# One decoder layer on one core: GELU calls two steps apart, GELU rounding on GpSimd, earlier reads of softmax sums

## The chip, the cores and the metric

The kernel runs on one core of one Trainium2 chip. The core has TensorE (PE in the profile; its weight loads are PEld), VectorE (DVE), ScalarE (ACT), GpSimd (POOL) and SyncE (SP), each with an instruction stream of its own, and DMA queues. The metric is the device time in microseconds, the median of several runs; lower is better.

## The reference

A batch of 16 sequences of 512 tokens with 256 features goes through attention and a feed-forward part, each with a layer norm behind it:

```
q = query @ wq + query @ Aq @ Bq * 4;  k = query @ wk;  v = query @ wv + query @ Av @ Bv * 4
q, k = rope(q), rope(k)                      # 16 heads of 16
attn = softmax(causal(q k^T / 4));  x = layernorm(query + (attn v) @ wo)
h = butterfly(x @ W_exp + b_exp, up)         # 1024 hidden, 10 stages, linear
h = gelu(h + up_bias)
y = butterfly(h, down) @ W_con + b_con + down_bias
out = layernorm(x + y)
```

The butterflies are linear, so the kernel folds them into two dense matrices, W1 (256 x 1024) and W2 (1024 x 256), once at the start.

## The kernel before, in words

All work of a batch is cut into pieces, and a function `steps` writes out by hand the order of the pieces. Every engine walks the same list and does the pieces that are its own, in order, so an engine that waits in one piece holds back all its later ones. An iteration `i` has 20 steps (`t`), and each step does the scores of one quarter of a head group; pieces of the neighbouring batches (`i+1`, `i-1`, `i-2`) are laid between them. Iterations 3 to 14 run as a loop, the rest is written out.

Products that need float32 accuracy are made of three matmul passes on rounded parts: a high part, rounded by ScalarE, and a low part, the rest, subtracted by VectorE or GpSimd (`mm3`).

The pieces that the change and the steps below touch, by name:

- S: scores of a step (L564, L590), from which VectorE takes the maxima (L869, L874); every fifth step it rounds them into `m_pad` (L883, L885), MT transposes them, ScalarE copies them to `m_row`, MOUT stores and MROW reads them back on SP (L464, L468).
- ST: the scores transposed (L602), for steps later by the lead of S; ScalarE exponentiates them into `pT` (L743), and GpSimd zeroes what lies behind the diagonal (SEL, L1026). There are three PSUM banks for two halves a step, so ST of a step waits for the first exp of the step before. PV multiplies with the values (L637).
- RAW stores a group's raw sums and outputs, SMOC reads back the sums `s_m` and the outputs `o_c` (L480, L482), RCP takes reciprocals on VectorE (L906), REC stores them (L485), RB reads them back spread over the partitions (L493), and ON multiplies on GpSimd (L1041). Each has two halves, 0 and 1; WO, the output projection (L647), needs both.
- WO's result is added to the input on VectorE (L911); LNS, LNA and LNB are the statistics, the aggregate with a power on GpSimd (L1045), and the scaling of a layer norm; BIAS adds a bias on GpSimd (L1051).
- XT transposes the normed rows (L653); ScalarE and VectorE split them (L774, L897); W1 expands (L522), and its eight tiles are read out by ScalarE (even, L820) and VectorE (odd, L914).
- GE is one GELU call over half of the hidden units (L826). GHI rounds a piece of the result (ScalarE, L794) into `x1T_hi`, GLO makes its low part (L919) in `x1T_lo`, and W2 and W2B contract the first and the second half (L669); W2E adds the rest of the layer (L933). The high and low buffers hold one piece for each half, so a piece waits for the W2 of the piece before it.
- ROPE, HIGH and LOW rotate and split the heads of the next batch (GpSimd L1035, L1036, ScalarE L770, GpSimd L373); QKH, QKL store them and FILL reads them back on SP; XRES reads the residual; XTL, XHI, XLO load and split the batch after that; V makes the values of the next batch.

Of the kernel before, what the change touches and what calls it, by code (L numbers as in the profile page):

```python
# [52 lines left out]
def steps(i, static):  # L53
# [19 lines left out]
    second = {2: ("MT", i, 1), 7: ("MT", i, 2), 12: ("MT", i, 3), 17: ("MT", i + 1, 0), 14: ("XT", i - 1, 0)}
    third = {14: ("XT", i - 1, 1)}
    for n in range(1, NHT):
        (first if n % 2 else third)[16 + (n - 1) // 2] = ("W1", i - 1, n)
    for n in range(NHT):
        (first if n > 1 else third)[2 + n] = ("W2B" if n % 2 else "W2", i - 2, n // 2)
    for t in range(NU):
# [35 lines left out]
        if t == 18:  # L115
            put("LNB", i - 2, 3)
# [25 lines left out]
        if t == 19:  # L142
            put("GE", i - 1, 1)
# [61 lines left out]
def layer(nc, xT_d, x_d, wqk_d, wv_d, lora_d, wo_d, wexpT_d, upin_d, dnin_d, wx_d, bx_d, wcon_d,  # L205
          bout_d, cs_d, ident_d, mask_d, out_d):
    ctx = ExitStack()
    with ctx:
# [623 lines left out]
        def _(dve):  # L832
# [26 lines left out]
            def one(step):  # L859
# [56 lines left out]
                elif kind == "GLO":  # L916
                    tile, half = n // 2, n % 2
                    dve.wait_ge(ghi_done, NHT * b + n + 1)
                    dve.tensor_tensor(g_lo[:, half, :, :],  # L919
                                      gact[:, NHT // 2 * half:NHT // 2 * (half + 1),  # L920
                                           tile * P:(tile + 1) * P],
                                      g_hi[:, half, :, :].bitcast(FP32), ALU.subtract)\
                       .then_inc(glo_done, 1)
# [79 lines left out]
        def _(pool):  # L1003
# [7 lines left out]
            def one(step):  # L1011
# [158 lines left out]
```

## Time and profile before

| | |
|---|---|
| median of 3 runs | 1574.66 us (1572.19 to 1581.97) |
| the profiled execution's own time | 1588.03 us |
| its span | 1586.3 us |
| PE busy | 1275.8 us, 80% |
| DVE busy | 971.9 us, 61% |
| ACT busy | 768.3 us, 48% |
| POOL busy | 491.5 us, 31% |
| mean granted clock of TensorE | 0.883 |

The span runs from the first to the last instruction of one profiled execution, which was slower than the median of the runs. Busy shares are means over the whole span. The granted clock is a share of 2.4 GHz: 0.5 is 1.2 GHz throughout a stretch, 1.0 is 2.4. A tile's name on the left of an arrow is written, on the right read; the second buffers for the GELU parts lie in those of the normed rows, so GHI and GLO carry the names `x1T_hi` and `x1T_lo`.

### The profile page before, as it was taken

To read this page: it belongs to the slowest core of one execution; us is meant where nothing else is said; L and a number is where in the kernel's file an instruction comes from. 1 tells how busy PE (TensorE), PEld (TensorE's weight loads), DVE (VectorE), ACT (ScalarE), POOL (GpSimd) and SP (SyncE) were. 2 spreads that over 40 slices of the span, in tenths; PEclk is the share of its full clock that TensorE was granted. 3 is DMA by queue.
4 is the path that set the end of the run, shared out by engine and by line. 5 is a ranking of instruction groups with operands and counts; after the bars stand their busy time and mean duration, and the time that the engine had idled before them with its cause. 6 is when DMAs were issued, how large, how long until landed. Compare 5 with 4: busy or idle time off the path is not lost.

```text
span 1586.3 us, 27377 instructions
## 1 busy us (share of the span) xinstructions
PE 1275.8 (80%) x8328; PEld 820.5 (52%) x8328; DVE 971.9 (61%) x2024; ACT 768.3 (48%) x1259; POOL 491.5 (31%) x520
## 2 busy tenths in 40 slices
PE   3677888888878888887888888788887888879766
PEld 2433445555555555555555645555555555545355
DVE  6689555665656567565656656655665666566333
ACT  1366454553636455363645536364553636464512
POOL 3124233242323324242332424233242423322210
PEclk8878899998989989898899989889898989998888
DMA  5744534253343525334342533435253343522110
GB/s 199 174 116 129 136 89 122 63 156 84 109 122 93 145 62 154 81 109 131 96 135 62 155 81 102 127 86 156 62 150 84 102 128 92 150 75 64 34 43 27
DMA packets 94983, 169.89 MB, mean 107 GB/s; under 512 B 14872, under 2 KB 36120, under 8 KB 94944
## 3 DMA queue, kind: packets, MB, share of 16 engines
q1 hardware_dynamic: 93888, 166.53, 38.3%
q10 hardware_dynamic: 832, 1.83, 0.3%
q0 software_dynamic: 224, 1.04, 0.2%
q8 instruction: 21, 0.34, 0.1%
q14 instruction: 18, 0.15, 0.0%
HBM read 92.28 MB, written 77.07 MB: 107 GB/s over the span
## 4 chain that ended last, share of the span: by engine, by line
PE 50%; issue 17%; DVE 14%; ACT 11%; DMA 4%; POOL 3%; ACTq 0%; SPq 0%; DVEq 0%; POOLq 0%
PE ps_m L522 16%; PE ps_m L669 8%; PE ps_o L637 7%; PE ps_m L647 6%; PE ps_t L602 5%; DVE m_raw L874 4%; ACT pT L743 3%; PE ps_s L564 3%; PE ps_s L590 3%; ACT L743 2%; DVE x1T_lo L919 2%; PE ps_m L653 1%; POOL o_c L1041 1%; DVE rope_in L893 1%; ACT L826 1%
## 5 line engine op out<-in xcount | busy, mean ns | idle before, releaser
L743 ACT ACTIVATE pT<-ps_t 128x512 f32<-128x512 f32 x640 | 346.9, 595 | 475.8 <-PE ps_t L602 474.7
L874 DVE TENSOR_REDUCE m_raw<-ps_s 128x1 f32<-128x512 f32 (+2 forms) x768 | 344.7, 503 | 157.0 <-PE ps_s L590 154.5
L1026 POOL TENSOR_SCALAR_AFFINE_SELECT pT<-pT 128x512 f32<-128x512 f32 (+1 forms) x320 | 188.8, 592 | 744.5 <-ACT pT L743 744.4
L602 PE MATMUL ps_t<-q_st,k_st 50*128 50x512 f32 (+3 forms) x1024 | 177.1, 405 | 75.3 <-ACT pT L743 68.6
L637 PE MATMUL ps_o<-pT,v_aug 128*32 128x512 f32 (+3 forms) x2048 | 212.8, 490 | 7.2 <-issue 7.2
L919 DVE TENSOR_TENSOR x1T_lo<-gact,x1T_hi 128x512 fp32r<-128x512 f32 x128 | 124.7, 976 | 128.5 <-ACT x1T_hi L794 126.7
L564 PE MATMUL ps_s<-k_st,q_st 48*128 48x512 f32 (+3 forms) x1024 | 142.9, 338 | 66.6 <-DVE m_raw L874 46.6
L602 PEld LDWEIGHTS ps_t<-q_st,k_st 50*128 50x128 f32 x1024 | 86.1, 195 | 176.9 <-ACT pT L743 82.2
L647 PE MATMUL ps_m<-wo,o_c 128*128 128x256 f32 x256 | 90.0, 513 | 73.2 <-POOL o_c L1041 73.2
L564 PEld LDWEIGHTS ps_s<-k_st,q_st 48*128 48x128 f32 x1024 | 103.4, 204 | 79.9 <-DVE m_raw L874 54.9
L669 PE MATMUL ps_m<-w_hi,x1T_hi 128*128 128x256 f32 x512 | 95.7, 310 | 43.1 <-DVE rope_in L893 18.8
L590 PE MATMUL ps_s<-maskb,identb 128*128 128x256 bf16 (+1 forms) x640 | 118.5, 269 | 0.0
L669 PEld LDWEIGHTS ps_m<-w_hi,x1T_hi 128*128 128x128 f32 x512 | 70.4, 193 | 87.6 <-issue 47.0
L647 PEld LDWEIGHTS ps_m<-wo,o_c 128*128 128x128 f32 x256 | 62.6, 257 | 101.0 <-POOL o_c L1041 60.3
L522 PE MATMUL ps_m<-x1T_hi,w_hi 128*128 128x512 f32 x256 | 100.2, 476 | 12.2 <-DVE x1T_lo L897 10.9
L794 ACT ACTIVATE x1T_hi<-gact 128x512 fp32r<-128x512 f32 x128 | 80.4, 630 | 56.6 <-PE ps_m L669 56.6
L911 DVE TENSOR_TENSOR x_res<-ps_m,x_res 128x512 f32<-128x512 f32 x32 | 22.1, 691 | 133.9 <-PE ps_m L647 133.9
L914 DVE TENSOR_SCALAR gact<-ps_m,gbias 128x512 f32<-128x512 f32 x64 | 48.0, 750 | 85.3 <-PE ps_m L522 85.1
L869 DVE TENSOR_REDUCE m_raw<-ps_s 128x2 f32<-128x512 f32 x128 | 81.9, 681 | 10.2 <-PE ps_s L590 9.8
L373 POOL TENSOR_TENSOR rot<-rot,rot_hi 128x1024 f32<-128x1024 f32 x28 | 66.6, 2380 | 67.9 <-ACT rot_hi L770 67.9
L820 ACT ACTIVATE gact<-ps_m,gbias 128x512 f32<-128x512 f32 x64 | 44.0, 688 | 86.4 <-PE ps_m L522 86.4
L522 PE MATMUL ps_m<-x1T_lo,w_hi 128*128 128x512 f32 x256 | 85.3, 416 | 0.0
(119 smaller groups left out, 2063.5 us busy)
## 6 DMA issues: line engine op xcount, KB each, us to landing
qk_scr<-rot_hi SPq DMA_DIRECT2D x64, 512.0 KB, 3.6
q_st<-qk_scr SPq DMA_DIRECT2D x128, 192.0 KB, 4.5
k_st<-qk_scr SPq DMA_DIRECT2D x128, 192.0 KB, 4.9
qk_scr<-rot SPq DMA_DIRECT2D x32, 512.0 KB, 3.2
o_scr<-o_raw SPq DMA_DIRECT2D x64, 256.0 KB, 2.1
r_b<-in_xT SPq DMA_DIRECT2D x17, 512.0 KB, 3.4
o_c<-o_scr SPq DMA_DIRECT2D x32, 256.0 KB
r_b<-r_scr SPq DMA_DIRECT2D x32, 256.0 KB
```

The lines of the kernel that those rows point to most:

```text
L522: mm = pe.matmul(out, w[a][k], x[c][k], start=(j == 0 and k == 0), stop=(j == 2 and k == n - 1))
L564: return pe.matmul(ps_s[:, r, off:off + (qt + 1) * P], q_st[rows, pr, qt * P:(qt + 1) * P], k_st[rows, pr, 0:(qt + 1) * P], start=start, s ...
L590: pe.matmul(o, identb[:, :], m, start=False, stop=True, skip_group_check=True).then_inc(s_done, 1)
L602: return pe.matmul(ps_t[:, ST_BANK[2 * n + r], off:off + (NT - kt) * P], k_st[rows, pr, kt * P:(kt + 1) * P], q_st[rows, pr, kt * P:T], st ...
L637: mm = pe.matmul(ps_o[32 * j:32 * j + 32, q0:q1], v_aug[:, kt, GH * g + j, :], src, start=(c == 0), stop=(c == 3), skip_group_check=True)
L647: mm = pe.matmul(pm[:, j * D:(j + 1) * D], o_c[:, k, t * P:(t + 1) * P], wo[:, k, :], start=(k == 0), stop=(k == KD - 1))
L669: mm = pe.matmul(pm[:, 0:D], (g_hi, g_lo)[a][:, half, k, :], (w2_hi, w2_lo)[c][:, NHT // 2 * half + k, :], start=(half + j + k == 0), stop ...
L743: act.activation(pT[:, g % 2, slot, half * T:(half + 1) * T], ps_t[:, ST_BANK[2 * n + r], :], ACT.Exp, scale=SCALE).then_inc(exp_done, 1)
L869: ins = dve.tensor_reduce(m_raw[:, r, :, 1], ps_s[:, r, :].rearrange("p (x c) -> p x c", x=GP), AX.X, ALU.max, negate=True)
L874: ins = dve.tensor_reduce(m_raw[:, r, u // 2, qt:qt + 1], ps_s[:, r, off:off + (qt + 1) * P], AX.X, ALU.max, negate=True)
L919: dve.tensor_tensor(g_lo[:, half, :, :], gact[:, NHT // 2 * half:NHT // 2 * (half + 1), tile * P:(tile + 1) * P], g_hi[:, half, :, :].bitc ...
L1026: pool.affine_select(out=v, in_=v, compare_op=ALU.is_ge, fill=0.0, base=0, pattern=pattern, channel_multiplier=-1).then_inc(mask_done, 1)
```

## The change

What moves, by piece (step before, step now):

- the second GELU call from behind the exps of step 19 to behind those of step 0 of the next iteration, and with it GHI, GLO, W2, W2B and W2E one step later each (W2 of the first tile 2 to 3);
- GLO from VectorE to GpSimd;
- SMOC of half 1 in front of its step's transfers, RCP and REC of half 1 from step 8 to 7, in front of LNS and of MOUT, RB of it from 8 to 7 behind MOUT, ON of it from 10 to 9, and RCP and REC of half 0 from 19 to 18; XRES of half 1 from 9 to 10;
- V from steps 10 and 13 to 13 and 14, XT from 14 to 15 with one transpose on either side of ST and S, W1 from 15 to 19 into 16 to 19, two a step;
- the first statistics (LNS) of the first layer norm ahead of WO's second result, and the last of the second from 15 to 14.

```diff
     first = {0: ("QK", i + 1, 0), 1: ("QK", i + 1, 1), 2: ("QK", i + 1, 2), 3: ("QK", i + 1, 3),
-             10: ("V", i + 1, 0), 11: ("WO", i - 1, 0), 12: ("WO", i - 1, 1), 13: ("V", i + 1, 1),
-             15: ("W1", i - 1, 0)}
...
+             11: ("WO", i - 1, 0), 12: ("WO", i - 1, 1), 13: ("V", i + 1, 0), 14: ("V", i + 1, 1),
+             15: ("XT", i - 1, 0)}
...
-        if 1 <= t <= NHT:
-            put("GHI", i - 2, t - 1)
-            put("GLO", i - 2, t - 1)
+        if 2 <= t < 2 + NHT:
+            put("GHI", i - 2, t - 2)
+            put("GLO", i - 2, t - 2)
         if t == 6:
-            put("LNS", i - 2, 2)
-        if t == 8:
+            put("SMOC", i - 1, 1)
+        if t == 7:
             put("RCP", i - 1, 1)
             put("REC", i - 1, 1)
+            put("LNS", i - 2, 2)
-        if t == 10:
+        if t == 9:
             put("ON", i - 1, 1)
...
         if t == 18:
             put("GE", i - 1, 0)
-        if t == 19:
-            put("GE", i - 1, 1)
+        if t == 0:
+            put("GE", i - 2, 1)
...
+                elif kind == "GLO":
+                    tile, half = n // 2, n % 2
+                    pool.wait_ge(ghi_done, NHT * b + n + 1)
+                    pool.tensor_tensor(g_lo[:, half, :, :],
+                                      gact[:, NHT // 2 * half:NHT // 2 * (half + 1),
+                                           tile * P:(tile + 1) * P],
+                                      g_hi[:, half, :, :].bitcast(FP32), ALU.subtract)\
+                       .then_inc(glo_done, 1)
```

The line numbers of the changed kernel are lower by 4 in the first half of the engines' code, and GLO stands at L1034. GpSimd in steps 2 and 3 of the loop, before (LOW, then ON; the selections are SEL):

```order
L1026 AFFINE_SELECT pT<-pT 128x2x256
L372 REGISTER_ALU
L373 TENSOR_TENSOR rot<-rot,rot_hi 128x1024
L393 ISA
L1026 AFFINE_SELECT pT<-pT 128x2x128
L1039 ISA
L1041 TENSOR_TENSOR o_c<-o_c,r_b 128x512
```

and now, from the selection of step 1 on:

```order
L1014 AFFINE_SELECT pT<-pT 128x2x256
L1033 ISA
L1034 TENSOR_TENSOR x1T_lo<-gact,x1T_hi 128x512
L368 REGISTER_ALU
L369 TENSOR_TENSOR rot<-rot,rot_hi 128x1024
L389 ISA
L1014 AFFINE_SELECT pT<-pT 128x2x128
L1033 REGISTER_ALU
L1034 TENSOR_TENSOR x1T_lo<-gact,x1T_hi 128x512
L1027 ISA
L1029 TENSOR_TENSOR o_c<-o_c,r_b 128x512
```

A subtraction of the GELU part (GLO) now stands ahead of LOW and of ON, and so on in each step to the ninth.

SyncE behind the fetches of the next batch's first group, before (steps 8 and 9: MROW's two reads, then REC, RB, XRES):

```order
L468 DMA q_st<-m_scr 2x1024
L468 ISA
L468 DMA q_st<-m_scr 2x1024
L393 REGISTER_ALU
L485 ISA
L485 DMA r_scr<-r_m 64x64
L393 REGISTER_ALU
L493 DMA r_b<-r_scr 128x1x512
L425 ISA
L425 DMA x_res<-in_x 128x2x256
```

and now (steps 6 and 7: XRES, then REC, MOUT, RB):

```order
L421 DMA x_res<-in_x 128x2x256
L389 REGISTER_ALU
L481 ISA
L481 DMA r_scr<-r_m 64x64
L389 REGISTER_ALU
L460 ISA
L460 DMA m_scr<-m_row 32x128
L389 REGISTER_ALU
L489 DMA r_b<-r_scr 128x1x512
L389 REGISTER_ALU
```

The store of the reciprocals went ahead of the maxima's store and of the fetches, and their spread read ahead of the fetches and of the maxima's reads.

ScalarE at the end of the loop, before (the exps of step 18, GELU, the exps of step 19, GELU):

```order
L743 ACTIVATE pT<-ps_t 128x512
L819 REGISTER_ALU
L820 ACTIVATE gact<-ps_m,gbias 128x512
L826 ACT_TABLE_LOAD
L826 ACTIVATE gact<-gact 128x2048
L742 ISA
L743 ACT_TABLE_LOAD
L743 ACTIVATE pT<-ps_t 128x512
L742 REGISTER_ALU
L743 ACTIVATE pT<-ps_t 128x512
L826 ACT_TABLE_LOAD
L826 ACTIVATE gact<-gact 128x2048
```

and now at the loop's head (behind the copy OE of the outputs: the exps of step 0, GELU, the first exp of step 1):

```order
L738 ISA
L739 ACTIVATE pT<-ps_t 128x512
L738 REGISTER_ALU
L739 ACTIVATE pT<-ps_t 128x512
L820 ISA
L822 ACT_TABLE_LOAD
L822 ACTIVATE gact<-gact 128x2048
L738 ISA
L739 ACT_TABLE_LOAD
L739 ACTIVATE pT<-ps_t 128x512
```

The second call left the end of the loop and stands one step's exps, and the copy of the outputs, further on.

## Rows read from the trace of the kernel before

**Rows 1.** Windows: one iteration; us, busy (x count) PE, PEld, DVE, ACT, POOL, clock, DMA.

```profile
778.80:871.60 92.80, 77.27 (x516) 49.97 (x516) 58.21 (x120) 46.36 (x76) 30.57 (x32) 0.91 0.40 109
```

**Rows 2.** Table of waits, whole run: who <- whom: us in total, times, longest.

```profile
PE ps_m L647 <- POOL o_c L1041: 73.2, 16, 6.1
...
PE ps_t L602 <- ACT pT L743: 68.6, 33, 3.8
...
PE ps_s L564 <- DVE m_raw L874: 46.6, 30, 3.6
...
PE ps_m L669 <- DVE rope_in L893: 18.8, 13, 1.9
...
PE ps_m L669 <- DVE x1T_lo L919: 17.2, 30, 4.3
```

**Rows 3.** Timeline, steps 6 to 11: start, us, engine, line, what; idle before, releaser.

```profile
715.36 0.67 SPq L480 DMA_DIRECT2D s_m<-o_scr  x1
...
719.77 0.54 DVE L906 RECIPROCAL r_m<-s_m 64x64 f32<-64x64 f32 x1
...
723.33 0.66 SPq L468 DMA_DIRECT2D q_st<-m_scr  x2
...
724.32 0.59 SPq L485 DMA_DIRECT2D r_scr<-r_m  x1
...
727.03 0.67 SPq L493 DMA_DIRECT2D r_b<-r_scr  x1
...
731.14 1.26 POOL L1041 TENSOR_TENSOR o_c<-o_c,r_b 128x512 f32<-128x512 f32 x1 [5.84 <-DMA r_b<-r_scr]
...
732.45 3.43 PE L647 MATMUL ps_m<-wo,o_c 128*128 128x256 f32 x8 [4.97 <-POOL o_c L1041]
```

**Rows 4.** Timeline around the GELU calls, one iteration and the end of another.

```profile
689.80 0.55 PE L602 MATMUL ps_t<-q_st,k_st 50*128 50x128 f32 x4 [3.15 <-ACT pT L743]
...
771.35 1.92 ACT L826 ACTIVATE gact<-gact 128x2048 f32<-128x2048 f32 x1
...
775.71 0.50 PE L602 MATMUL ps_t<-q_st,k_st 50*128 50x512 f32 x2 [1.42 <-ACT pT L743]
...
776.97 1.91 ACT L826 ACTIVATE gact<-gact 128x2048 f32<-128x2048 f32 x1
```

**Rows 5.** Windows, columns as in rows 1, of three stretches behind holes.

```profile
690.00:697.30 7.30, 6.08 (x31) 2.85 (x29) 6.34 (x11) 4.00 (x9) 4.05 (x4) 0.77 0.73 144
732.40:736.00 3.60, 3.55 (x12) 2.68 (x12) 0.00 (x0) 0.00 (x0) 0.36 (x1) 0.58 0.78 170
750.60:755.00 4.40, 4.40 (x15) 2.98 (x16) 0.50 (x2) 1.44 (x3) 0.00 (x0) 0.50 0.75 174
```

**Rows 6.** By line: GpSimd and VectorE (ns min/median/max; the page's rows: busy, mean).

```profile
L1036 POOL TENSOR_TENSOR rot<-rope_in x32: 1258/1282/1745, 21.9 to 1353.5; 128x512 f32<-128x512 f32 x32
...
L919 DVE TENSOR_TENSOR x1T_lo<-gact,x1T_hi x128: 677/692/2470, 225.9 to 1575.7; 128x512 fp32r<-128x512 f32 x128
...
L1026 POOL TENSOR_SCALAR_AFFINE_SELECT pT<-pT 128x512 f32<-128x512 f32 (+1 forms) x320 | 188.8, 592 | 744.5 <-ACT pT L743 744.4
...
L373 POOL TENSOR_TENSOR rot<-rot,rot_hi 128x1024 f32<-128x1024 f32 x28 | 66.6, 2380 | 67.9 <-ACT rot_hi L770 67.9
```

**Rows 7.** Timeline: first W2 matmuls of step 4 and of step 7.

```profile
704.56 0.73 PE L669 MATMUL ps_m<-w_hi,x1T_hi 128*128 128x256 f32 x4 [0.42 <-DVE y L933]
...
714.89 0.73 PE L669 MATMUL ps_m<-w_hi,x1T_hi 128*128 128x256 f32 x4 [0.49 <-DVE x1T_lo L919]
```

**Rows 8.** Timeline: S behind the layer norm, and the first W1.

```profile
747.19 0.50 PE L564 MATMUL ps_s<-k_st,q_st 48*128 48x512 f32 x2 [2.11 <-DVE m_raw L874]
...
750.59 1.19 PE L522 MATMUL ps_m<-x1T_hi,w_hi 128*128 128x512 f32 x2 [0.79 <-DVE x1T_lo L897]
```

**Rows 9.** Timeline: GpSimd's addition and VectorE's cast beside it.

```profile
757.97 2.42 POOL L1051 TENSOR_TENSOR x_res<-x_res,bias_out 128x1024 f32<-128x1024 f32 x1
...
759.25 1.18 DVE L883 CAST m_pad<-m_raw 128x16 fp32r<-128x16 f32 x1
```

More of the change, by code:

```diff
@@ L70, in steps @@
     first = {0: ("QK", i + 1, 0), 1: ("QK", i + 1, 1), 2: ("QK", i + 1, 2), 3: ("QK", i + 1, 3),
-             10: ("V", i + 1, 0), 11: ("WO", i - 1, 0), 12: ("WO", i - 1, 1), 13: ("V", i + 1, 1),
-             15: ("W1", i - 1, 0)}
[L73 to L76, printed above, removed]
+             11: ("WO", i - 1, 0), 12: ("WO", i - 1, 1), 13: ("V", i + 1, 0), 14: ("V", i + 1, 1),
+             15: ("XT", i - 1, 0)}
+    second = {2: ("MT", i, 1), 7: ("MT", i, 2), 12: ("MT", i, 3), 17: ("MT", i + 1, 0), 15: ("XT", i - 1, 1)}
+    third = {3: ("W2", i - 2, 0)}
     for n in range(NHT):
-        (first if n > 1 else third)[2 + n] = ("W2B" if n % 2 else "W2", i - 2, n // 2)
+        (third if n % 2 else first)[16 + n // 2] = ("W1", i - 1, n)
+        if n:
+            first[3 + n] = ("W2B" if n % 2 else "W2", i - 2, n // 2)
     for t in range(NU):
@@ L93, in steps @@
                 put("MROW", b, n)
-        if 1 <= t <= NHT:
-            put("GHI", i - 2, t - 1)
-            put("GLO", i - 2, t - 1)
+        if 2 <= t < 2 + NHT:
+            put("GHI", i - 2, t - 2)
+            put("GLO", i - 2, t - 2)
         if t == 6:
-            put("LNS", i - 2, 2)
-        if t == 8:
+            put("SMOC", i - 1, 1)
+        if t == 7:
             put("RCP", i - 1, 1)
             put("REC", i - 1, 1)
-        if t == 10:
+            put("LNS", i - 2, 2)
+        if t == 9:
             put("ON", i - 1, 1)
+        if t == 12:
+            put("LNS", i - 1, 0)
         if t == 13:
@@ L108, in steps @@
             put("LNB", i - 1, 1)
-        if t == 15:
             put("LNS", i - 2, 3)
@@ L115, in steps @@
         if t == 18:
+            put("RCP", i, 0)
+            put("REC", i, 0)
             put("LNB", i - 2, 3)
@@ L122, in steps @@
         if t == 12:
-            put("LNS", i - 1, 0)
             put("LNS", i - 1, 1)
@@ L131, in steps @@
                     put("MOUT", table[t][1], table[t][2])
-                if table[t][0] == "W2B":
-                    put("W2E", *table[t][1:])
         if u >= 1:
@@ L155, in steps @@
         if t == 6:
-            put("SMOC", i - 1, 1)
             put("XRES", i - 1, 0)
         if t == 7:
+            put("RB", i - 1, 1)
             put("FILL", i + 1, 0)
-        if t == 8:
-            put("RB", i - 1, 1)
-        if t == 9:
+        if t == 10:
             put("XRES", i - 1, 1)
-        if t == 10:
             put("FILL", i + 1, 1)
@@ L178, in steps @@
             put("OUT", i - 2)
-            put("RCP", i, 0)
-            put("REC", i, 0)
         put("SEL", i, t)
@@ L915, in one @@
                        .then_inc(evac_w1[1], 1)
[L916 to L923, printed above, removed]
                 elif kind == "DM":
```

## The prediction

> **What bounds the kernel now.** I read the busy times by iteration first, then the table of waits, then the timeline of one iteration. One iteration of the steady loop (one batch) takes 92.8 us, of which TensorE's matmuls are busy 77.3, VectorE 58.2, ScalarE 46.4 and GpSimd 30.6 [rows 1]. TensorE is the bound, with 15.5 us of holes per batch, and some of its busy time is run at a lower clock. The table of waits names the holes over the whole run: 73.2 us (16 times, once a batch) in which the output projection WO waits for GpSimd's scaled `o_c`, 68.6 us (33 times, two a batch) in which the transposed scores ST wait for a score bank that ScalarE's exps have not read, 46.6 us in which the scores S wait for the maxima, and 36.0 us (18.8 and 17.2) ahead of the contracting matmuls W2 [rows 2]. Of the 15.5 us a batch these are nearly all.
>
> The timeline shows how the two large ones come about. WO: the sums are read back at 715.36, the reciprocal runs at 719.77, but its store is issued only at 724.32, behind the transfers of the maxima rows at 723.33 in SP's order; the spread reciprocals are fetched at 727.03, GpSimd multiplies at 731.14 to 732.40, and WO starts at 732.45 after a wait of 4.97 [rows 3]. GELU: two calls of 1.9 us with a table load on either side start at 771.35 and 776.97, with just one step's exps between them; ST waits 1.42 at 775.71, and, at the same place of the iteration before, 3.15 at 689.80 for the second [rows 4]. After each large hole the granted clock is low: 0.77 over 690.0 to 697.3 and 0.58 over 732.4 to 736.0, so part of that time is at 1.2 GHz instead of 2.4, after TensorE had stood idle [rows 5].
>
> **The change part by part.**
>
> *Reads of sums and reciprocals (SMOC, RCP, REC, RB, ON).* Nothing is added; the same transfers go earlier. From the read of the sums to the end of the multiply the chain took 17.0 us: 4.4 to the reciprocal, 4.55 from there to the store, 2.7 to the fetch, 4.1 to its landing [rows 3]. With the store ahead of its step's MOUT the 4.55 falls to about 0.7, since the reciprocal itself is 0.54 long; the fetch then stands behind one MOUT, worth at most a microsecond. The reciprocal is one step earlier, in front of LNS, GLO and a step's maxima, and the read of the sums no longer stands behind the last low part of the rotated heads: another 2 to 4 us. So `o_c` is ready 6 to 8 us sooner against a wait of 5, and the wait goes, with 1 to 3 us to spare. ON also stands behind the last GLO on GpSimd, which eats 1.28 of it [rows 6]. What is late next is TensorE itself, with W2 of the last tile in the place of V. Queued behind the new waits: VectorE's reciprocal now stands ahead of a step's maxima and waits for the sums; they were there 4.4 us after issue without a wait being shown, so its cost is between 0 and about 2 us a batch; I take 0, because half a step or more lies between. XRES, FILL and MROW on SP come later by the fetch's wait (RB waits some 2 us for the store); MROW is bound by its own landing, so 0 to 1 us, and I take 0. Gain: 73.2 less the last batch's 6.1, where nothing is left to cover it, 67; and the clock: 3.55 us busy at 0.58 is 3.55 x 0.42 = 1.5 us a batch [rows 5], x 15 = 22. Together **-89**.
>
> *GELU two steps apart.* The same two calls and four table loads a batch. A call with its loads holds ScalarE for 1.28 + 1.92 + 1.28 = 4.5 us. ST of a step needs the first exp of the step before, so a hole of 4.5 us after a step's exps is hidden if TensorE has more than that before the ST after the next. After the first call it has S, two W1 tiles and PV, ST, S, another W1, PV and QK: some 9 us. After the second (now behind ST of step 0) it has S, QK, ST, S, PV, QK: about 6.5. Both cover it, the second barely, so I leave 0.5 us a batch (8) and take 68.6 - 8 = 61; from 690.0 to 697.3 TensorE was busy 6.08 us at 0.77, 6.08 x 0.23 = 1.4 a batch [rows 5], x 15 = 21. Together **-82**. The price: the second half's first high part (GHI) moves a step later, and W2 with it.
>
> *Low rounding (GLO) on GpSimd.* VectorE loses 8 calls a batch of 692 ns median; GpSimd gains 8. The nearest rows are its addition of the same shape, 1282 median and 1745 at most, and its 128x1024 subtraction at 2380, half of which is 1190 [rows 6]: I take 1.28, bounds 1.19 and 1.75. GpSimd's 30.6 us a batch become 41, so it is no bound over the batch, but it is over steps 2 to 6. Between the end of the first GLO and that of the fifth, it must do in order: LOW, SEL, GLO, ON, SEL, GLO, two rotations (ROPE), SEL, GLO, LOW, SEL, GLO, which is 2 x 2.38 + 4 x 0.59 + 4 x 1.28 + 3 x 1.28 = 16.1 us, and about 1 us (an estimate) in which LOW waits for ScalarE's HIGH: 17.1. TensorE from the same point to the W2 that takes the fifth low part needs 2 us to reach the first W2 (estimate), 2.0 for it with its PV, and three steps: 704.56 to 714.89 is 10.33, less 0.49 of wait 9.84 [rows 7]: 13.8. So W2 waits some **3 us a batch** for GpSimd, x 15 = +45, bounds 0 and 6. That these 3 us also lower the clock is as likely as not (after 1.42 of wait it stayed, after 3.15 it fell): +1.4 x 15 / 2 = +11. The old waits ahead of W2, 36.0, go: the bank is free earlier and VectorE's queue is no longer in the way. In the last two iterations W2 is a bare chain, longer by 1.28 - 0.69 for each of four tiles: +5. Together **+25**.
>
> The GPSIMD Engine Reference of the Trainium skill (section Engine selection) speaks against this edit: elementwise work of two inputs belongs on VectorE and is about twice as slow on GpSimd. The trace agrees, 1282 against 692 ns, 1.85 times. At twice 692 the calls would be 0.10 us longer each, the stretch 0.4 us, the sum 6 us worse.
>
> *V later, layer norms spread (V, XT, W1, LNS).* No work changes. With V now on both sides of S1 the wait of 2.11 for the maxima behind the layer norm [rows 8] is covered by the 1.5 us of a V pair, but the S between the two transposes then waits for the statistics LNS put in front of its predecessor's maxima: I leave 1 us, a gain of 1.1 x 15 = 17. The second transpose now ends right ahead of W1, and its low part is queued on VectorE behind four maxima (1.4 us) : the wait of 0.79 [rows 8] becomes some 1.7, x 15 = +14, bounds 0 and 2.5 a batch. The slow stretch behind it (0.50 over 750.6 to 755.0 [rows 5]) I leave as it is. Together **-3**. The move of the other half's RCP and REC by a step I put at nothing: ON of that half is not what WO waits for.
>
> **The sum.** -89 - 82 + 25 - 3 = -149 against the profiled execution's own 1588.03 us (its span 1586.3 and 1.7 around it): 1439. The median of the three runs, 1574.66, is 0.9916 of the profiled time, so the forecast is 1439 x 0.9916 = **1427 us**, 9.4% less.
>
> **Rivals.**
>
> *GpSimd sets the pace more than I think.* VectorE's tiny operations on SBUF are held while GpSimd works: the 128x16 cast at 759.25, 0.17 us long elsewhere, took 1.18 and ended with GpSimd's addition of 757.97 to 760.39; a GLO of 692 ns took up to 2470 [rows 6, 9]. GpSimd will be near full in steps 2 to 8, so GLOs of 1.63 (5 x 0.35 = 1.75) and 2.4 us of held casts ahead of MT would add 4.2 us a batch, 62 in all: 1501 x 0.9916 = 1488. For it: how full those steps are; against: the longest holder, VectorE's own GLO, leaves that port. The SBUF — State Buffer page of the Trainium skill (section SBUF: two separate sides) gives the rule: the two engines' shared port pair is an exclusive lock for a whole instruction. The trace agrees, by the cast that ends with the addition. Chance 0.17.
>
> *The reciprocals are still late.* If the sums land later than the reciprocal's new place, or the fetch stays behind MOUT, half of the 89 stays: 1483.5 x 0.9916 = 1471. Chance 0.08.
>
> *The GELU hole only moves, so that the change doesn't do what it says.* The second call waits for the last W1 that VectorE adds its bias to, now behind the maxima of the last step; if that is late by 2 us, ST of step 2 waits and half of 82 stays: 1468. Chance 0.06.
>
> *Faster.* GpSimd keeps up after all (TensorE reaches W2 later than I reckon): the 45 and 11 go, 1383 x 0.9916 = 1371. Chance 0.09.
>
> *Slower than before.* One mechanism: GLO itself on GpSimd. It reads `gact` in four pieces of 128 elements, 512 apart, and writes the rounded type. Five GLOs stand in the stretch that sets the pace, so from 149 / 15 / 5 = 2.0 us more each, that is at 3.3 us, the gain is gone; at 4.0 us it is 1439 + 5 x 2.72 x 15 = 1643, x 0.9916 = 1629. Against it: SEL, with strided pieces too, takes 0.59 [rows 6]. Chance 0.02.
>
> **How the numbers follow.** The forecast has 0.58. Its own range is some 35 us either way (bounds of the W2 wait, 0 and 6 us a batch, are 45 us each way, but not all terms are at their ends together). Leaving out the outer half of the faster and the pacing rivals, the range is 1390 to 1490. Within 1% of before is what a measurement here can hardly tell from no change; it needs two or three rivals at once: 0.03. Slower by over 1%: 0.02. Faster by over 1%: 0.95.
>
> **What the new profile would show.** Right: the iteration at 81 to 84 us; WO's wait on `o_c` near 0 outside the last batch; ST's wait for exps under 10 us in all; GLO at 1.2 to 1.4 us on GpSimd, and W2's wait for it the longest hole on TensorE, 2 to 4 us a batch; W1 after the transposes waiting 1 to 2 us; the clock near 1 around WO and W2. Wrong: GLO above 1.6 us, WO still waiting for `o_c`, the wait of S or of ST's maxima rows grown by several us a batch, or VectorE's casts held at the maxima of steps 6 and 11.

## The result, and the profile after

The changed kernel took 1411.1 us, the median of 4 runs (1407.79 to 1418.86), against 1573.9 (1572.19 to 1581.97): a ratio of 0.8966, 95% interval 0.8924 to 0.9008. The forecast was 1427, 9.4% less; it is 10.3% less.

The page of the changed kernel's profile, busy time by engine:

```profile
PE 1214.9 (86%) x8328; PEld 790.2 (56%) x8328; DVE 844.4 (60%) x1896; ACT 756.9 (54%) x1259; POOL 633.5 (45%) x648
```

Windows of the changed kernel, one iteration, columns as in [rows 1]:

```profile
702.25:780.66 78.41, 71.72 (x517) 47.16 (x516) 49.25 (x112) 45.55 (x75) 39.76 (x40) 0.98 0.47 130
```

An iteration takes 78.4 us instead of 92.8 (forecast 81 to 84), at a mean clock of 0.98 instead of 0.91. TensorE runs the same number of matmuls over the same data, but is busy 60.9 us less over the run (1275.8 to 1214.9): that part of the gain is clock, the rest is waits. That it is clock shows in the product of busy time and the run's mean granted clock, which hardly moves: 1275.8 x 0.883 = 1126.5 before, 1214.9 x 0.928 = 1127.4 now. The profiled execution took 1407.79 us (span 1406.0) where that of before took 1588.03. The spans are 180.3 apart, so 119.4 of it are waits.

The waits of TensorE in the changed kernel, columns as in [rows 2]:

```profile
PE ps_m L665 <- POOL x1T_lo L1034: 44.2, 35, 4.8
PE ps_t L598 <- DMA q_st<-m_scr: 34.4, 15, 4.4
PE ps_m L518 <- DVE x1T_lo L893: 26.6, 16, 2.0
...
PE ps_s L560 <- DVE m_raw L870: 11.7, 13, 1.9
PE ps_t L598 <- ACT pT L739: 11.0, 19, 1.2
...
PE ps_m L643 <- POOL o_c L1029: 2.9, 1, 2.9
```

Against [rows 2]: WO's wait for `o_c` fell from 73.2 to 2.9, that of ST for the exps from 68.6 to 11.0, that of S for the maxima from 46.6 to 11.7. W2 waits 44.2 for GpSimd instead of 36.0 for VectorE. One large row the prediction had put at nothing: ST waits 34.4 us, once a batch, for `q_st<-m_scr`, the maxima rows MROW. In the kernel before that was 6.4.

The clock is read from the groups by line (busy, mean ns of one; then idle before them). Kernel before: the values' PV, the first pass of W1, WO and XT:

```profile
L637 PE MATMUL ps_o<-pT,v_aug 128*32 128x512 f32 (+3 forms) x2048 | 212.8, 490 | 7.2 <-issue 7.2
...
L522 PE MATMUL ps_m<-x1T_hi,w_hi 128*128 128x512 f32 x256 | 100.2, 476 | 12.2 <-DVE x1T_lo L897 10.9 <-DVE gact L914 1.3
...
L647 PE MATMUL ps_m<-wo,o_c 128*128 128x256 f32 x256 | 90.0, 513 | 73.2 <-POOL o_c L1041 73.2
...
L653 PE MATMUL ps_m<-ident,x_res 128*128 128x128 f32 x128 | 28.2, 395 | 8.1 <-DVE x_res L955 8.1
```

and the changed kernel's, same order:

```profile
L633 PE MATMUL ps_o<-pT,v_aug 128*32 128x512 f32 (+3 forms) x2048 | 199.0, 462 | 1.9 <-issue 1.9
...
L518 PE MATMUL ps_m<-x1T_hi,w_hi 128*128 128x512 f32 x256 | 94.0, 449 | 27.7 <-DVE x1T_lo L893 26.6 <-ACT gact L816 1.1
...
L643 PE MATMUL ps_m<-wo,o_c 128*128 128x256 f32 x256 | 69.0, 418 | 2.9 <-POOL o_c L1029 2.9
...
L649 PE MATMUL ps_m<-ident,x_res 128*128 128x128 f32 x128 | 21.4, 294 | 6.5 <-DVE x_res L943 6.5
```

WO's mean falls from 513 to 418 ns, PV's from 490 to 462, XT's from 395 to 294, at equal counts.

### The profile page after: what moved, and what is told of

The parts are those of the page before. It is cut to its first block, busy times and chain, and to the rows that moved or that the text cites. A ratio compares the mean times of both kernels' runs of the same rounds, so it can differ in the third digit from the quotient of the medians.

```text
span 1406.0 us, 27389 instructions
## 1 busy us (share of the span) xinstructions
PE 1214.9 (86%) x8328; PEld 790.2 (56%) x8328; DVE 844.4 (60%) x1896; ACT 756.9 (54%) x1259; POOL 633.5 (45%) x648
## 4 chain that ended last, share of the span: by engine, by line
PE 52%; DVE 9%; issue 9%; DMA 9%; ACT 8%; POOL 8%; SPq 3%; ACTq 0%; POOLq 0%; DVEq 0%
PE ps_m L518 20%; PE ps_t L598 7%; PE ps_o L633 7%; DMA q_st<-m_scr 5%; PE ps_m L665 5%; PE ps_m L643 5%; PE ps_s L560 4%; PE ps_s L586 3%; DVE m_raw L870 3%; ACT pT L739 3%; POOL x1T_lo L1034 3%; DMA r_scr<-r_m 2%; SPq L455 2%; POOL pT L1014 2%; ACT L822 2%
## 5 line engine op out<-in xcount | busy, mean ns | idle before, releaser
L1014 POOL TENSOR_SCALAR_AFFINE_SELECT pT<-pT 128x512 f32<-128x512 f32 (+1 forms) x320 | 176.8, 553 | 586.3 <-ACT pT L739 586.3
L598 PE MATMUL ps_t<-q_st,k_st 50*128 50x512 f32 (+3 forms) x1024 | 178.9, 409 | 45.6 <-DMA q_st<-m_scr 34.4
L633 PE MATMUL ps_o<-pT,v_aug 128*32 128x512 f32 (+3 forms) x2048 | 199.0, 462 | 1.9 <-issue 1.9
L1034 POOL TENSOR_TENSOR x1T_lo<-gact,x1T_hi 128x512 fp32r<-128x512 f32 x128 | 164.0, 1282 | 33.3 <-ACT x1T_hi L790 33.0
L665 PE MATMUL ps_m<-w_hi,x1T_hi 128*128 128x256 f32 x512 | 96.5, 312 | 45.3 <-POOL x1T_lo L1034 44.2
L518 PE MATMUL ps_m<-x1T_hi,w_hi 128*128 128x512 f32 x256 | 94.0, 449 | 27.7 <-DVE x1T_lo L893 26.6
L816 ACT ACTIVATE gact<-ps_m,gbias 128x512 f32<-128x512 f32 x64 | 43.7, 683 | 137.4 <-PE ps_m L518 137.4
L921 DVE TENSOR_TENSOR y<-ps_m,x_res 128x256 f32<-128x256 f32 x64 | 27.2, 425 | 142.6 <-PE ps_m L665 142.6
L665 PE MATMUL ps_m<-w_hi,x1T_lo 128*128 128x256 f32 x512 | 85.4, 292 | 0.0
L665 PE MATMUL ps_m<-w_lo,x1T_hi 128*128 128x256 f32 x512 | 84.3, 289 | 0.0
L518 PE MATMUL ps_m<-x1T_hi,w_lo 128*128 128x512 f32 x256 | 82.0, 402 | 0.0
L586 PEld LDWEIGHTS ps_s<-maskb,identb 128*128 128x128 bf16 x640 | 37.0, 98 | 68.7 <-issue 46.2
```

The costliest lines, as they stand in the source:

```text
L518: mm = pe.matmul(out, w[a][k], x[c][k], start=(j == 0 and k == 0), stop=(j == 2 and k == n - 1))
L586: pe.matmul(o, identb[:, :], m, start=False, stop=True, skip_group_check=True).then_inc(s_done, 1)
L598: return pe.matmul(ps_t[:, ST_BANK[2 * n + r], off:off + (NT - kt) * P], k_st[rows, pr, kt * P:(kt + 1) * P], q_st[rows, pr, kt * P:T], st ...
L633: mm = pe.matmul(ps_o[32 * j:32 * j + 32, q0:q1], v_aug[:, kt, GH * g + j, :], src, start=(c == 0), stop=(c == 3), skip_group_check=True)
L665: mm = pe.matmul(pm[:, 0:D], (g_hi, g_lo)[a][:, half, k, :], (w2_hi, w2_lo)[c][:, NHT // 2 * half + k, :], start=(half + j + k == 0), stop ...
L1014: pool.affine_select(out=v, in_=v, compare_op=ALU.is_ge, fill=0.0, base=0, pattern=pattern, channel_multiplier=-1).then_inc(mask_done, 1)
```

## The experiments

All ratios are against the kernel before, which ran beside each set of experiments; "expected" is the text on record. The median of the kernel before was 1576.9 us beside experiment 1, 1575.0 beside 2 to 4, 1565.5 beside 5 and 1573.1 beside 6, so a difference of some 10 us between medians of two sets can come from the set, and ratios are the better measure there. The edits are shown against the changed kernel, cut where "..." stands.

**1. Four parts undone, one at a time.** Theory A: each part is worth about what the prediction's term says, so that undoing it costs or gives that. Theory B: the parts cover for each other.

GLO back on VectorE (the same branch, moved from GpSimd's list to VectorE's):

```diff
                 elif kind == "GLO":
                     tile, half = n // 2, n % 2
-                    pool.wait_ge(ghi_done, NHT * b + n + 1)
-                    pool.tensor_tensor(g_lo[:, half, :, :],
+                    dve.wait_ge(ghi_done, NHT * b + n + 1)
+                    dve.tensor_tensor(g_lo[:, half, :, :],
```

> The changed kernel with GLO alone put back on VectorE (same steps). Theory A (each part is worth its own hole on TensorE, and GLO on GpSimd is the one part that costs): the 44 us in which W2 waits for GLO and the low clock behind them go, the kernel gets faster than the changed one, 1360 to 1385 us, and the wait of W2 for VectorE's GLO stays under 20 us. Theory B (relieving VectorE is what lets the rest work): maxima, casts and the normalisation queue behind GLO again, 1420 to 1450 us, with the waits of S for its maxima up from 12 to 40 us or more.

Measured 1440.7 (1438.2 to 1445.0), ratio 0.9179 (0.9095 to 0.9264): 30 us slower, though W2 waits less. Its waits:

```profile
PE ps_t L598 <- DMA q_st<-m_scr: 64.9, 15, 5.2
...
PE ps_m L518 <- DVE rope_in L889: 22.7, 16, 3.9
PE ps_m L665 <- DVE x1T_lo L915: 19.4, 30, 4.2
```

W2's wait fell from 44.2 to 19.4, but the one for the maxima rows grew from 34.4 to 64.9, and the projections QK now wait 22.7 (7.4 before the edit) for VectorE to read out the rotations. The timeline says why. In this kernel, the store of the raw outputs and the ST that waits for the rows:

```profile
1140.21 0.38 SPq L469 DMA_DIRECT2D o_scr<-o_raw  x1
...
1162.02 0.80 PE L598 MATMUL ps_t<-q_st,k_st 50*128 50x512 f32 x2 [4.50 <-DMA q_st<-m_scr]
```

and in the changed kernel at the same place:

```profile
1113.30 0.39 SPq L469 DMA_DIRECT2D o_scr<-o_raw  x1
...
1135.31 0.49 PE L598 MATMUL ps_t<-q_st,k_st 50*128 50x512 f32 x2 [2.54 <-DMA q_st<-m_scr]
```

From the store to ST it is 21.8 us in the one and 22.0 in the other. Over eight or nine steady iterations each of these two kernels, of the two below that put the GELU call back and V, XT, W1 and LNS back, and of those of experiments 3 and 4, it is never under 20.9 or over 22.4. That chain sets the pace of these steps, so W2 waiting 1.7 us less inside it only lets ST wait longer at its end. The 30 us come mainly from two other places: QK waits 15.3 more, in the steps ahead of the store, where the chain can't hide it; and behind ST's longer wait the clock is low (ST's two matmuls take 0.80 instead of 0.49), so that WO's matmuls take 89.0 us in the run instead of 69.0, while W2's take 9.0 less (257.2). Neither theory had that: A's sign was wrong, and B's number was right by another mechanism (S waits 11.5, no more than before).

The second GELU call back at step 19:

```diff
-        if t == 0:
-            put("GE", i - 2, 1)
+        if t == 19:
+            put("GE", i - 1, 1)
```

> The changed kernel with the second GELU call alone put back behind the exps of step 19; GHI, GLO and W2 keep their later steps. Theory A: the wait of ST for exps comes back from 11 to 60 or more, and the low clock behind it, some 82 us: 1470 to 1500. Theory B (TensorE is paced elsewhere, by GpSimd in steps 2 to 6, and takes up the hole there): 1411 to 1440, with W2's wait for GLO falling as ST's rises.

Measured 1460.9 (1458.4 to 1465.0), ratio 0.9293 (0.9210 to 0.9377): 50 us slower, between the theories. One of the two holes comes back, 2.28 behind the second call, where the changed kernel has 0.52; none stands behind the first, where the kernel before has 1.42:

```profile
719.04 1.92 ACT L822 ACTIVATE gact<-gact 128x2048 f32<-128x2048 f32 x1
...
725.24 1.92 ACT L822 ACTIVATE gact<-gact 128x2048 f32<-128x2048 f32 x1
...
729.60 0.55 PE L598 MATMUL ps_t<-q_st,k_st 50*128 50x128 f32 x4 [2.28 <-ACT pT L739]
```

The reads and reciprocals back (SMOC behind the transfers, RCP, REC and RB in step 8, ON in 10; the other half's RCP and REC from 18 to 19):

```diff
-        if t == 6:
-            put("SMOC", i - 1, 1)
         if t == 7:
-            put("RCP", i - 1, 1)
-            put("REC", i - 1, 1)
             put("LNS", i - 2, 2)
+        if t == 8:
+            put("RCP", i - 1, 1)
+            put("REC", i - 1, 1)
...
-        if t == 9:
+        if t == 10:
             put("ON", i - 1, 1)
...
         if t == 6:
+            put("SMOC", i - 1, 1)
             put("XRES", i - 1, 0)
         if t == 7:
-            put("RB", i - 1, 1)
             put("FILL", i + 1, 0)
+        if t == 8:
+            put("RB", i - 1, 1)
```

> The changed kernel with SMOC, RCP, REC, RB and ON of both halves alone put back to the steps of before (XRES and LNS stay where the change has them, since W2 is a step later). Theory A: WO waits for the scaled outputs again, 60 to 80 us in all, with 1.2 GHz behind it, 89 us: 1485 to 1505, and ST's wait for the maxima rows (34 us) falls, since the fetch no longer stands ahead of them, which takes up to 30 us off: 1455 to 1505. Theory B: the wait comes back by half or less, 1411 to 1450.

Measured 1462.8 (1458.9 to 1465.2), ratio 0.9306 (0.9220 to 0.9393): 52 us slower, as A said. WO waits 71.4 in all again, and the wait for the maxima rows shrinks from 34.4 to 7.2. GpSimd's multiply and WO, with the waits that [rows 3] has:

```profile
682.65 1.26 POOL L1030 TENSOR_TENSOR o_c<-o_c,r_b 128x512 f32<-128x512 f32 x1 [5.12 <-DMA r_b<-r_scr]
...
683.97 3.78 PE L644 MATMUL ps_m<-wo,o_c 128*128 128x256 f32 x8 [4.73 <-POOL o_c L1030]
```

The eight matmuls behind that wait take 3.78 us; in the changed kernel they take 1.89.

V, XT, W1 and LNS back:

```diff
-             11: ("WO", i - 1, 0), 12: ("WO", i - 1, 1), 13: ("V", i + 1, 0), 14: ("V", i + 1, 1),
-             15: ("XT", i - 1, 0)}
-    second = {2: ("MT", i, 1), 7: ("MT", i, 2), 12: ("MT", i, 3), 17: ("MT", i + 1, 0), 15: ("XT", i - 1, 1)}
-    third = {3: ("W2", i - 2, 0)}
+             11: ("WO", i - 1, 0), 12: ("WO", i - 1, 1), 13: ("V", i + 1, 1), 15: ("W1", i - 1, 0)}
+    second = {2: ("MT", i, 1), 7: ("MT", i, 2), 12: ("MT", i, 3), 17: ("MT", i + 1, 0), 14: ("XT", i - 1, 0)}
+    third = {3: ("W2", i - 2, 0), 10: ("V", i + 1, 0), 14: ("XT", i - 1, 1)}
...
-        (third if n % 2 else first)[16 + n // 2] = ("W1", i - 1, n)
+        if n:
+            (first if n % 2 else third)[16 + (n - 1) // 2] = ("W1", i - 1, n)
...
-        if t == 12:
-            put("LNS", i - 1, 0)
```

> The changed kernel with V, XT, W1 and the LNS calls alone put back to the steps of before (V's first part behind the scores of step 10). Theory A: nothing net, the wait of S comes back (from 12 to 40 us) and that of W1 for the second transpose falls (from 27 to 11): 1405 to 1430. Theory B (V at steps 13 and 14 covers more than the S wait, and the slow clock behind the layer norm comes back with it, some 2 us a batch): 1435 to 1460.

Measured 1467.1 (1465.2 to 1471.0), ratio 0.9346 (0.9259 to 0.9432): 56 us slower, beyond both. Its waits:

```profile
PE ps_s L560 <- DVE m_raw L870: 41.9, 27, 2.9
PE ps_t L598 <- ACT pT L739: 26.7, 32, 2.5
...
PE ps_m L518 <- DVE x1T_lo L893: 9.4, 16, 1.5
```

S waits 30 us more, ST 16 more for the exps (0.87 behind the first GELU call comes back), and W1 17 less for its low part. And the hole of 2.12 ahead of the transposes brings the low clock back, here S, the eight transposes and the first W1:

```profile
778.13 0.50 PE L560 MATMUL ps_s<-k_st,q_st 48*128 48x512 f32 x2 [2.12 <-DVE m_raw L870]
...
778.78 1.69 PE L649 MATMUL ps_m<-ident,x_res 128*128 128x128 f32 x8
...
781.97 1.19 PE L518 MATMUL ps_m<-x1T_hi,w_hi 128*128 128x512 f32 x2 [0.49 <-DVE x1T_lo L893]
```

Not in every iteration does it reach W1: at 700.90 the same pair takes 0.70, behind a hole of the same 2.12. Over the run the transposes take 26.7 us (21.4 in the changed kernel) and W1 266.2 (258.6).

**2. The maxima rows ahead of the fetches.** In the changed kernel, the timeline of steps 7 to 10:

```profile
732.45 0.59 SPq L481 DMA_DIRECT2D r_scr<-r_m  x1
...
733.37 0.35 SPq L460 DMA_DIRECT2D m_scr<-m_row  x1
...
734.49 0.67 SPq L489 DMA_DIRECT2D r_b<-r_scr  x1
...
735.58 0.34 SPq L455 DMA_DIRECT2D q_st<-qk_scr  x1
...
737.08 0.32 SPq L455 DMA_DIRECT2D k_st<-qk_scr  x1
...
737.64 0.66 SPq L464 DMA_DIRECT2D q_st<-m_scr  x2
...
739.42 1.29 POOL L1029 TENSOR_TENSOR o_c<-o_c,r_b 128x512 f32<-128x512 f32 x1 [0.95 <-DMA r_b<-r_scr]
...
742.76 0.50 PE L598 MATMUL ps_t<-q_st,k_st 50*128 50x512 f32 x2 [1.88 <-DMA q_st<-m_scr]
...
743.66 1.89 PE L643 MATMUL ps_m<-wo,o_c 128*128 128x256 f32 x8
```

SP issues in order: the spread read `r_b` at 734.49, behind it four fetches of the next batch's scores from 735.58 to 737.08, and only then MROW at 737.64, 4.27 us behind the store of the maxima (at 751.44 and 753.01 of this iteration, where nothing lies between, it is 1.57). ST waits 1.88 for it. The edit puts the fetches behind MROW:

```diff
         if t == 7:
             put("RB", i - 1, 1)
+        if t == 8:
             put("FILL", i + 1, 0)
```

> The changed kernel with the fetch of the next batch's first head group (FILL 0) put one step later on SP, behind the reads of the maxima rows (MROW) of step 8. Theory A: the 34 us in which ST waits for these rows come from their standing behind four fetches; they are issued some 2.4 us earlier a batch, the wait falls under 10 us: 1380 to 1395. Theory B: the rows are bound by the landing of their own store; the wait stays over 25 us: 1405 to 1420.

Measured 1358.0 (1352.2 to 1358.4), ratio 0.8626 (0.8557 to 0.8696): 53 us faster than the changed kernel. The rows now follow the store after 2.17 us, with the fetch behind them:

```profile
702.90 0.35 SPq L461 DMA_DIRECT2D m_scr<-m_row  x1
...
704.15 0.67 SPq L490 DMA_DIRECT2D r_b<-r_scr  x1
...
705.07 0.71 SPq L465 DMA_DIRECT2D q_st<-m_scr  x2
...
706.21 0.32 SPq L456 DMA_DIRECT2D q_st<-qk_scr  x1
```

and ST's wait for them is gone, while W2's stays:

```profile
PE ps_m L666 <- POOL x1T_lo L1035: 46.9, 43, 4.8
...
PE ps_t L599 <- DMA q_st<-m_scr: 1.3, 2, 0.8
```

33 us are that wait; TensorE's busy time falls 20.5 as well (1214.9 to 1194.4), which is clock: WO's matmuls take 6.9 less, W2's 4.8. Theory A, beyond its price.

**3. Both transposes ahead of ST 15.**

```diff
-    second = {2: ("MT", i, 1), 7: ("MT", i, 2), 12: ("MT", i, 3), 17: ("MT", i + 1, 0), 15: ("XT", i - 1, 1)}
+    second = {2: ("MT", i, 1), 7: ("MT", i, 2), 12: ("MT", i, 3), 17: ("MT", i + 1, 0)}
...
+            if first[t][0] == "XT":
+                put("XT", i - 1, 1)
```

> The changed kernel with both transposes XT ahead of ST of step 15, instead of one on either side of ST and S. Theory A: W1's wait of 27 us comes from the second low part being queued behind four maxima; it falls to 10 or less, and S of step 15 may wait a little more: 1390 to 1402. Theory B: the time is only moved to S3 or to the layer norm's end: 1405 to 1420.

Measured 1397.0 (1393.5 to 1399.6), ratio 0.8878 (0.8808 to 0.8948): 14 faster, with an interval that overlaps the changed kernel's (0.8924 to 0.9008). W1's wait fell from 26.6 to 11.7, nearly to the 10 that A said; the wait for the maxima rows rose from 34.4 to 45.5. TensorE's idle time in all did not change (191.1 to 190.4 us); what the profiled execution gained, 8.2, is busy time, that is clock (1214.9 to 1207.4).

**4. Two of the eight GLOs on VectorE** (numbers 1 and 3, with a semaphore for each engine).

```diff
+ON_DVE = (1, 3)
...
+                elif kind == "GLO" and n in ON_DVE:
+                    dve.wait_ge(ghi_done, NHT * b + n + 1)
```

> The changed kernel with GLO 1 and 3 of each batch (the two behind which W2 waits) on VectorE, the other six on GpSimd. Theory A (GpSimd's queue in steps 2 to 6 is the pace): W2's wait of 44 us falls to 15 or less: 1375 to 1395. Theory B (VectorE's subtraction is held by GpSimd's operations as long as they run, and holds the maxima): no gain, 1405 to 1425.

Measured 1427.4 (1425.5 to 1428.9), ratio 0.9075 (0.9005 to 0.9145): 16 slower, the interval again touching the changed kernel's. W2's wait fell only to 36.4 (27.8 for GpSimd, 8.6 for VectorE), so A is out; the rows' rose to 49.1: the chain of experiment 1 again, and B's "no gain" only half by its mechanism: VectorE's two subtractions are held (1566 ns in the mean), but S waits just 4.0 more.

**5. The parts undone once more, with the fetches of experiment 2 moved.** There ST no longer waits for the rows, so that chain can't hide what a part does. Each is experiment 2's edit and one of the others.

> The kernel with FILL 0 behind MROW (1358 us), and GLO back on VectorE. Theory A' (GLO on GpSimd costs TensorE the 47 us of W2's wait; undoing it alone made the kernel slower only because ST then waited 65 us for the maxima rows that SP issued behind the fetches): without those fetches in front W2's wait falls to some 20 and nothing takes its place, 1325 to 1340. Theory B (VectorE relieved is worth some 30 us by itself): 1380 to 1395.

> The kernel with FILL 0 behind MROW (1358 us), and the second GELU call back behind the exps of step 19. Theory A': the GELU term is 82 us of which the wait for the maxima rows hid a third: 1430 to 1445, with ST's wait for exps over 55. Theory B (it is worth the 50 us that undoing it alone showed): 1400 to 1415.

> The kernel with FILL 0 behind MROW (1358 us), and both transposes ahead of ST of step 15. Theory A': the two waits are apart and both gains hold: 1338 to 1346. Theory B (the gain of one is eaten by the other as it was where the rows' wait grew from 34 to 46): 1352 to 1358.

> The kernel with FILL 0 behind MROW (1358 us), and V, XT, W1 and LNS back at the steps of before. Theory A': their part is worth what undoing it alone showed, 56 us or a little more, since the rows' wait had grown by 10 there: 1415 to 1425. Theory B (the forecast's 3 us, the rest an effect of the rows' wait): 1358 to 1375.

| experiment 2's kernel with | us (range) | ratio (95%) | against 1358.0 | by the ratios | TensorE's waits that moved, us |
|---|---|---|---|---|---|
| GLO on VectorE | 1348.9 (1343.4 to 1350.9) | 0.8592 (0.8533 to 0.8652) | -9 | -5 | W2 46.9 to 18.5, QK 7.3 to 22.7 |
| the GELU call back | 1394.3 (1388.9 to 1395.2) | 0.8896 (0.8838 to 0.8954) | +36 | +43 | ST for exps 11.8 to 37.2 |
| both XT ahead of ST 15 | 1341.1 (1339.9 to 1346.0) | 0.8552 (0.8496 to 0.8607) | -17 | -12 | W1 26.5 to 11.7 |
| V, XT, W1, LNS back | 1407.9 (1404.7 to 1413.4) | 0.8992 (0.8931 to 0.9053) | +50 | +58 | S 13.1 to 43.7, exps 11.8 to 27.7, W1 26.5 to 10.9 |

"By the ratios" is the difference to experiment 2's ratio, 0.8626 (0.8557 to 0.8696), times 1575 us. The two that put a part back are clear of noise. For GLO and for the transposes the intervals overlap with that of experiment 2, so their few us are not told from nothing by the times. The profiled executions have TensorE idle 161.8 us in experiment 2's kernel, 155.3 with GLO on VectorE and 143.0 with both transposes ahead; the busy time is 1194.4, 1193.9 and 1201.2.

So GLO on GpSimd costs 9 us by the medians and 5 by the ratios, if anything, not 25, and not -30; the GELU call is worth some 36 to 43; the transposes' saving in W1's wait stays, beside that of the fetches. Of the theories on record A' held for the transposes. GLO's time lies in neither range (nothing near the 30 us of B, and A' overlooked QK's wait); the GELU call is below both, nearer to B; V, XT, W1 and LNS lie between the two, nearer to A'.

**6. All three gains together**: the fetches behind MROW, both transposes ahead of ST 15, GLO on VectorE.

> The fetches FILL 0 stand behind the maxima rows MROW, both transposes XT ahead of ST 15, and the low rounding GLO is on VectorE again. If the gains add (A'), the 9 us that GLO on VectorE gave beside the moved fetches come on top of 1341: 1328 to 1338. Rival: VectorE is what the transposes' earlier place leans on (x1T_lo of the layer norm and the rounding of GELU's outputs share it), and the two gains cancel: 1341 to 1350, with W1's wait back above 20 us or the wait of QK for rope_in above 25.

Measured 1331.0 (1323.7 to 1332.1), ratio 0.8486 (0.8396 to 0.8577): within noise the gains add (A'), and it beats both kernels, the changed one by 5.7%. The rival's signs stayed away: W1's wait is 11.7 and QK's 22.7. Its waits:

```profile
PE ps_m L521 <- DVE rope_in L892: 22.7, 16, 3.9
...
PE ps_m L668 <- DVE x1T_lo L918: 19.4, 30, 4.2
...
PE ps_m L521 <- DVE x1T_lo L896: 11.7, 16, 1.5
```

## Why the prediction was right, and where not, step by step

The sum was -149 on the profiled execution and came out at -180.2. On the medians it was -148 and came out at -163; before's profiled execution was 14 us above its median, the changed kernel's 3 below, so half of the difference is that of executions. Of the signs of being wrong that the prediction names, one came in part: ST's wait for the maxima rows grew, by 1.9 us a batch. By terms, from the two tables of waits and the groups by line:

| term | forecast, us | measured on the profiles, us |
|---|---|---|
| WO's wait | -67 | -70.3 |
| ST's wait for exps | -61 | -57.6 |
| S's wait for the maxima | -17 | -34.9 |
| W2's waits (36.0 in [rows 2], 44.2 now) | -36 + 45 + 5 = +14 | +8.2 |
| W1's wait for the transposes | +14 | +15.7 |
| ST's wait for the maxima rows | 0 | +28.0 |
| other waits | 0 | -8.5 |
| clock, WO | -22 | -21.0 |
| clock, behind the GELU calls (PV, QK) | -21 | -23.2 |
| clock, transposes and W1 | 0 | -17.7 |
| clock, W2 | +11 | +3.1 |
| clock, other matmuls | 0 | -2.1 |

The clock rows are differences of busy time at equal counts: WO 90.0 to 69.0; PV 212.8 to 199.0 and the three passes of QK 143.0 to 133.6; XT 28.2 to 21.4 and W1's three passes 269.5 to 258.6; W2's 263.1 to 266.2. The waits came out at -119 where -117 was forecast, and the clock at -61 where -32 was. That the waits agree to 2 us is luck: the rows' +28.0, which the prediction put at nothing, was made up by S (17.9 better than forecast), by the other waits (8.5) and by W2 (5.8).

*Reads of sums and reciprocals: right.* The wait went, and with it the low clock behind it: WO starts at 743.66 without a wait of its own, at a granted clock of 1.00 (743.66 to 745.60). Undone, it costs 52 us, or 105 against experiment 2's kernel, where the rows aren't late either (that pair differs in the place of the fetches too); as I read it, the two differ because the late reads and the late rows hide one another.

*MROW: the step that failed.* The prediction had the four fetches queue behind the wait of RB and saw that MROW comes later, and then "MROW is bound by its own landing, so 0 to 1 us, and I take 0". MROW was bound by its place in SP's order: 2.7 us later than where nothing lies between, of which ST waits 1.9 in the shown iteration and 2.3 in the mean. With the clock, experiment 2 prices that place at 53 us. "What is late next is TensorE itself" was wrong for the same reason: late next is this chain, and while it is, a part that saves TensorE time inside it gives nothing, as experiments 1 and 4 show. The total came out inside the range all the same, since other terms gave more than their share.

*GELU: right in its waits, too large as a price for one call's move.* The holes went (-58), and the 0.5 us a batch that the prediction left over is there (0.52 behind the second call). But only the second hole comes back when the call is put back, and not whole: 2.28 us where the kernel before has 3.15. The first goes with the new order of V, XT and W1, as its return in that experiment shows (0.87 of 1.42). With the clock the move is worth some 36 to 43 (experiment 5), not 82: some of the 82 was the other part's.

*GLO on GpSimd: its duration right, the wait's size right by luck, its price too high.* The page's row of the changed kernel:

```profile
L1034 POOL TENSOR_TENSOR x1T_lo<-gact,x1T_hi 128x512 fp32r<-128x512 f32 x128 | 164.0, 1282 | 33.3 <-ACT x1T_hi L790 33.0
```

1282 ns, the value taken, and W2's wait for it 44.2 where 45 was worked out. But the prediction added up GpSimd's queue to the fifth low part, and there W2 does not wait (729.78 in this iteration). It waits for the second, behind LOW, and for the fourth, behind the two rotations:

```profile
717.22 0.74 PE L665 MATMUL ps_m<-w_hi,x1T_hi 128*128 128x256 f32 x4 [0.88 <-POOL x1T_lo L1034]
...
724.63 1.03 PE L665 MATMUL ps_m<-w_hi,x1T_hi 128*128 128x256 f32 x4 [1.68 <-POOL x1T_lo L1034]
```

The low clock behind the wait came, in eight of ten steady iterations (last section). Against the kernel before, whose W2 had waits of its own, W2's matmuls take only 3.1 more where 11 was forecast; experiment 1, which takes GLO off GpSimd, gives 9.0 of them back, experiment 5 gives 3.0. Putting GLO back gains only 5 to 9 us in experiment 5, since VectorE, with eight more calls, is late with the rotations' readout. The rival by which held casts pace the kernel did not come. Casts are held, 394 ns in the mean (line L879) where the shortest takes 174; but they were in the kernel before (432), with GLO on VectorE they are less so in experiment 1 (243), and the transposes MT behind them wait 1.0 us in the whole run. The SBUF — State Buffer page of the Trainium skill (section SBUF: two separate sides) has the two engines exclude one another on their shared port; the longer means agree with it, and GLO on VectorE shows the other side of it, in experiment 1 1017 ns in the mean where the median is 692.

*V, XT, W1, LNS: wrong in size, -3 for some -50.* S's wait fell by 35 where 17 was taken. And to leave "the slow stretch behind it" as it is was wrong: the 2.11 wait of S [rows 8] stood ahead of both the transposes and the first W1, and with it went their low clock, 17.7 us. W1's own wait of 1.67 at 761.39, which the prediction priced rightly at +14, did not lower it: its first two matmuls take 0.71, in [rows 8] 1.19. That it is the wait of S is shown by the experiment in which it comes back: transposes at 1.69, W1 at 1.19, and over the run 12.9 of the 17.7. Part of the size is the exps' wait that the GELU term had counted.

Left open: how far GLO on GpSimd is from setting the pace of steps 2 to 6 is known only from its removal; a kernel that does each GLO twice gave no time. Undoing GELU costs 50 with the late rows in place and 36 without (51 and 43 by the ratios); whether these differ isn't settled. The rows' wait is 13.0 longer there (47.4), and the chain of experiment 1 would account for it: inside it W2 waits 2.5 less and W2's matmuls take 9.7 less.

## What to carry to other kernels

When a transfer that waits is put forward in an in-order issue queue, list everything that now stands behind its wait, and price the small read among it that the bounding engine needs, rather than the transfer that was moved; here the cure was one line (53 us). When a hole goes, look for the next-latest chain across the same steps before crediting a further saving inside it: GLO on VectorE cost 30 us while the rows were late, and nothing that the times can tell when they were not. And price a hole together with the low-clock matmuls behind it, all of them up to the next full-speed row: here that was a third of the gain.

## What the hardware showed that was not expected

The length of one wait does not tell the clock behind it. In the changed kernel ST's wait of 1.88 is followed by WO at full speed (1.89 for eight matmuls; the granted clock is 1.00 from 742.70 to 750.00), while W2's shorter wait for the fourth low part is followed by either level in two iterations of one kernel (experiment 2's; four matmuls of 128x256, then the windows of the six us behind, columns as in [rows 1]):

```profile
770.58 1.23 PE L666 MATMUL ps_m<-w_hi,x1T_hi 128*128 128x256 f32 x4 [1.69 <-POOL x1T_lo L1035]
...
846.99 0.74 PE L666 MATMUL ps_m<-w_hi,x1T_hi 128*128 128x256 f32 x4 [1.69 <-POOL x1T_lo L1035]
```

```profile
770.58:776.58 6.00, 6.00 (x37) 4.59 (x38) 2.20 (x5) 1.93 (x4) 4.94 (x5) 0.72 0.77 241
846.99:852.99 6.00, 5.74 (x46) 4.08 (x46) 3.70 (x6) 1.97 (x4) 5.78 (x5) 1.00 0.76 237
```

1.23 against 0.74 for the same four matmuls, and a granted clock of 0.72 against 1.00. The matmuls right behind a wait don't show it either way: in another iteration they take 0.73 (694.22), and the clock is 0.50 from 696.00 to 698.00. Of ten steady iterations, each with this wait of 1.64 to 1.70, the clock fell in eight in the changed kernel, in two in experiment 2's, in all ten with both transposes ahead there, and in none with the GELU call put back in the changed kernel. What tells them apart stays open. So the clock's part of an edit doesn't follow its waits: it went from 20.5 us beside 33 of wait (experiment 2) to 0.5 when GLO left GpSimd (experiment 5, busy time 1194.4 to 1193.9), where W2's wait fell by 28 and QK's rose by 15; and with both transposes ahead W2's matmuls took 12.0 us more than without (261.4 to 273.4), beside 15 us less of W1's wait.
